# Half of an attention layer's probability tiles turned by DMA in place of TensorE

## What is computed

```python
xn = layernorm(x)                               # x: 8 x 512 x 256, float32
q, k, v = split(xn @ qkv_w.T)                   # 16 heads of 64
q, k = rope(q), rope(k)
scores = q @ k.T / 8 - p * log1p(a * |i - j|)   # p, a per head
attn = softmax(scores)                          # 512 x 512 for each batch and head
y = (attn @ v) @ out_w.T
x = x + y + moe(xn)                             # 16 experts, top 1, capacity 256
```

## Time and profile before

| | us |
|---|---|
| median of 3 runs | 1337.12 |
| lowest, highest | 1335.97, 1337.2 |
| the profiled execution | 1339.31 |
| its span | 1337.5 |
| TensorE busy in the span | 1216.2 (91%) |
| VectorE | 1098.9 (82%) |
| ScalarE | 985.9 (74%) |
| GpSimd | 798.0 (60%) |

### The profile page before, as it was taken

How to read it: one execution, slowest core, us unless ns; L and a number is a source line. 1 busy time by engine, 2 the same in 40 slices (tenths; PEclk the granted TensorE clock), 3 DMA queues, 4 the chain that set the end, 5 groups by cost and what they waited for, 6 DMA issues and landing times.

```text
span 1337.5 us, 33943 instructions
## 1 busy us (share of the span) xinstructions
PE 1216.2 (91%) x13412; PEld 938.0 (70%) x13412; DVE 1098.9 (82%) x2166; ACT 985.9 (74%) x1831; POOL 798.0 (60%) x628
## 2 busy tenths in 40 slices
PE   5630999997699999999999999999999999999995
PEld 5620788895267777777777777777777777777764
DVE  7864799994388888888888888888888888888894
ACT  2775688882388777777778777877778777877773
POOL 3044000001788887886788788877778887886600
PEclk9975899998899999999999999999999999999998
DMA  8625666661445444444553454355445444444411
GB/s 267 237 62 187 219 236 234 234 212 40 117 123 141 104 111 127 120 117 115 147 154 98 112 151 104 96 141 142 117 130 146 105 112 127 120 118 113 135 41 48
DMA packets 172685, 182.47 MB, mean 136 GB/s; under 512 B 78066, under 2 KB 150783, under 8 KB 172528
## 3 DMA queue, kind: packets, MB, share of 16 engines
q1 hardware_dynamic: 160256, 160.03, 41.9%
q0 software_dynamic: 4352, 12.41, 2.7%
q10 hardware_dynamic: 7920, 7.87, 2.0%
HBM read 109.12 MB, written 54.56 MB: 122 GB/s over the span
## 4 chain that ended last, share of the span: by engine, by line
PE 71%; ACT 1%; DMA 1%; issue 1%; DVE 1%; SPq 0%; ACTq 0%; DVEq 0%
PE ps_t L1307 17%; PE ps_o L1323 13%; PE ps_x L1263 13%; PE ps_s L1296 8%; PE ps_s L1297 8%; PE ps_x L1283 7%; PE ps_x L1273 6%; ACT prob L1111 1%; DMA kswap<-qk_dram 0%; DMA qk_dram<-parts 0%; DMA ot<-ctx_parts 0%; ACT proj L1073 0%; ACT prob L1073 0%; DVE ctx_parts L1193 0%; ACT pt_hi L1087 0%
## 5 line engine op out<-in xcount | busy, mean ns | idle before, releaser
L1172 DVE SCALAR_TENSOR_TENSOR pt_lo<-ps_t,pt_hi 128x1024 f16<-128x1024 f32 x256 | 312.6, 1221 | 129.1 <-ACT pt_hi L1087 129.1
L1207 DVE CUSTOM_DVE_ANT_0 neg<-ps_s,strips,score_scale 128x512 f32<-128x512 f32 x512 | 361.7, 743 | 8.1 <-PE ps_s L1297 8.0
L1111 ACT ACTIVATE prob<-neg,neg_max 128x512 f32<-128x512 f32 x512 | 362.6, 712 | 0.0
L1087 ACT ACTIVATE pt_hi<-ps_t 128x1024 f16<-128x1024 f32 x256 | 261.9, 1023 | 128.5 <-PE ps_t L1307 126.5
L1307 PE MATMUL ps_t<-ident,prob 128*128 128x128 f32 x2048 | 269.4, 273 | 4.3 <-ACT prob L1111 4.2
L1307 PEld LDWEIGHTS ps_t<-ident,prob 128*128 128x128 f32 x2048 | 234.3, 141 | 39.1 <-issue 10.6
L1323 PE MATMUL ps_o<-val_hi,pt_hi 128*128 128x64 f16 x2048 | 206.0, 193 | 1.8 <-DVE pt_lo L1172 1.7
L1323 PE MATMUL ps_o<-val_hi,pt_lo 128*128 128x64 f16 x2048 | 206.2, 193 | 0.0
L1323 PE MATMUL ps_o<-val_lo,pt_hi 128*128 128x64 f16 x2048 | 206.2, 193 | 0.0
L1296 PE MATMUL ps_s<-qk 128*128 128x512 f16 x512 | 195.4, 382 | 6.0 <-DMA kswap<-qk_dram 5.6
L1297 PE MATMUL ps_s<-kswap,qk 128*128 128x512 f16 x512 | 194.9, 381 | 0.0
(11 more groups left out here) (186 smaller groups left out, 2565.0 us busy)
## 6 DMA issues: line engine op xcount, KB each, us to landing
raw<-in_L_ffn_w_dram SPq DMA_DIRECT2D x32, 1024.0 KB, 5.1
qk_dram<-parts SPq DMA_DIRECT2D x128, 256.0 KB
qk<-qk_dram SPq DMA_DIRECT2D x32, 1024.0 KB, 5.6
kswap<-qk_dram SPq DMA_DIRECT2D x64, 256.0 KB, 6.5
xa<-in_L_attn_x_dram SPq DMA_DIRECT2D x8, 512.0 KB, 6.4
xt_dram<-xth SPq DMA_DIRECT2D x8, 512.0 KB, 5.1
slots_dram<-zeros SPq DMA_DIRECT2D x4, 1024.0 KB, 8.3
xa<-slots_dram SPq DMA_DIRECT2D x16, 256.0 KB, 5.3
```

Source lines behind the costliest of these rows:

```text
L1087: nc.scalar.activation(pt[0][:, (l - 1) % 2].rearrange("p q k c -> p q (k c)"), ps_t[l % 2][:], ACT.Copy, scale=P_SCALE).then_inc(turned_h ...
L1111: nc.scalar.activation(prob[:, l % 2, q, :], neg[:, l % 2, q, :], ACT.Exp, bias=neg_max[:, 2 * (l % 2) + q:2 * (l % 2) + q + 1], scale=-1. ...
L1172: nc.vector.scalar_tensor_tensor(out=pt[1][:, (l - 1) % 2].rearrange("p q k c -> p q (k c)"), in0=ps_t[l % 2][:], scalar=P_SCALE, in1=pt[0 ...
L1207: nc.vector.tensor_tensor_reduce(neg[:, l % 2, q, :], ps_s[q][:], strips[:, h, start:start + S], score_scale[:, 0:1], 3.0e38, ALU.add, ALU ...
```

## The change

- In the odd slots but the last (127 of 256) the probabilities are not transposed by TensorE. ScalarE splits off their high half from `prob` into `prob_parts` (`prob_high`), VectorE the low half (`prob_low`, in slot s+1), and SP turns both in one DMA transpose of 2048 float16 a partition into `pt` (`turn_probs`). `prob_parts` has one buffer. The even slots go through TensorE as before.
- The values of a slot are taken three slots later, not two; `pair_lo` of a slot three slots later.
- `neg` is gone: reductions write to `prob` and the exponentials work in place, in a ring of three. `pt` has three buffers and holds both halves.
- `rot` holds one of the two rotations, so `step` splits each right after it is rotated. In the first two fills VectorE does so too.
- SP's list is written by groups, with `move` in two halves, `move_out` at the start of the next group and `move_in` after the second turn in it, and the context's transpose after the third.

The diff, cut to its core:

```diff
+DMA_TURNS = (1, 3, 5, 7)
...
-        rot = sb("rot", [P, 2, 2, S])
+        rot = sb("rot", [P, 2, S])
...
-        neg = sb("neg", [P, 2, 2, S])
         neg_max = sb("neg_max", [P, 4])
-        prob = sb("prob", [P, 2, 2, S])
+        prob = sb("prob", [P, 3, 2, S])
         sums = sb("sums", [P, 2, 8])
         rsum = sb("rsum", [P, 8])
-        pt = [sb(f"pt_{n}", [P, 2, 2, TPB, P], F16) for n in ("hi", "lo")]
+        pt = sb("pt", [P, 3, 2, 2, TPB, P], F16)
+        prob_parts = sb("prob_parts", [P, 2, 2, S], F16)
...
+        def by_dma(s):
+
+            return s % 8 in DMA_TURNS and s < NB * PAIRS - 2
+
+        def dma_slots(s):
+
+            return sum(by_dma(i) for i in range(s))
+
+        def pe_slots(s):
+
+            return s - dma_slots(s)
...
-            def move(n, r):
+            def move_out(n, r):
 
                 F = 2 * n + r
-                wait(sp, scored, 16 * (F - 1))
                 sp.wait_ge(parts_lo, 2 * F + 2)
                 for h in range(HG):
                     sp.dma_start(qk_dram[r, :, :, :, :, h, :].rearrange("w a f d s -> d (w a f) s"),
                                  parts[32 * h:32 * h + 32].rearrange("p w a f s -> p (w a f) s")).then_inc(parts_written, 16)
+
+            def move_in(n, r):
...
+            def turn_probs(s):
+
+                n = dma_slots(s)
+                wait(sp, pv_done, s - 2)
+                sp.wait_ge(prob_lo, n + 1)
+                sp.dma_start_transpose(pt[:, s % 3].rearrange("p a q k c -> p (a q k) c"),
+                                       prob_parts[:].rearrange("p a q s -> p (a q s)")).then_inc(turned_by_dma, 16)
...
+            def group(b, j):
+                first = PAIRS * b + 8 * j
+                before = divmod(4 * b + j - 1, 4)
+                if first:
+                    turn_probs(first - 1)
+                    if ahead(*before):
+                        move_out(*ahead(*before)[:2])
+                turn_probs(first + 1)
+                if first + 8 < NB * PAIRS:
+                    move_in((4 * b + j + 1) // 2, (j + 1) % 2)
+                if j == 1 and not is_last(b):
+                    load_routes(b + 1)
+                turn_probs(first + 3)
+                if first:
+                    turn_context(*before)
+                turn_probs(first + 5)
+                if j == 1 and not is_last(b):
+                    sp.wait_ge(filled, fills_before(b, 14))
+                    load_x(b + 1)
...
             def step(F, fills):
                 for w in range(2):
                     rotate(F, w, fills + 2 * w + 2)
-                for w in range(2):
                     if F > 1:
                         high(F, w)
                     low(F, w)
...
             def pair_hi(b, l):
-                act.wait_ge(turned, pairs_turned(b, l))
-                wait(act, pv_done, PAIRS * b + l - 2)
-                nc.scalar.activation(pt[0][:, (l - 1) % 2].rearrange("p q k c -> p q (k c)"), ps_t[l % 2][:],
+                s = PAIRS * b + l - 1
+                act.wait_ge(turned, pe_slots(s) + 1)
+                wait(act, pv_done, s - 2)
+                nc.scalar.activation(pt[:, s % 3, 0].rearrange("p q k c -> p q (k c)"), ps_t[pe_slots(s) % 2][:],
                                      ACT.Copy, scale=P_SCALE).then_inc(turned_hi, 1)
 
-            def context_hi(b, l):
-
-                unit = PAIRS // 4 * b + (l - 6) // 4
-                two = (l - 6) // 4 % 2
+            def prob_high(s):
+                n = dma_slots(s)
+                act.wait_ge(exp_done, 2 * s + 2)
+                wait(act, turned_by_dma, 16 * n)
+                nc.scalar.activation(prob_parts[:, 0], prob[:, s % 3], ACT.Copy, scale=P_SCALE).then_inc(prob_hi, 1)
...
+                if s % 4 == 3 and s >= 7:
+                    context_hi(s // 4 - 1)
                 if kind:
                     read_fill(kind, fills_before(b, l))
-                if l or not is_first(b):
-                    pair_hi(b, l)
                 for q in range(2):
                     act.wait_ge(negated, 2 * s + q + 1)
-                    if q == 0:
-                        wait(act, turned, pairs_turned(b, l - 1))
-                    nc.scalar.activation(prob[:, l % 2, q, :], neg[:, l % 2, q, :], ACT.Exp,
+                    nc.scalar.activation(prob[:, s % 3, q, :], prob[:, s % 3, q, :], ACT.Exp,
                                          bias=neg_max[:, 2 * (l % 2) + q:2 * (l % 2) + q + 1], scale=-1.0,
                                          accum_out=sums[:, l // 4 % 2, 2 * (l % 4) + q:2 * (l % 4) + q + 1]).then_inc(exp_done, 1)
-                if l % 4 == 2 and not (is_first(b) and l == 2):
-                    context_hi(b, l)
+                if by_dma(s):
+                    prob_high(s)
+                if s and not by_dma(s - 1):
+                    pair_hi(b, l)
...
-            def pair_lo(b, l):
-                dve.wait_ge(turned_hi, pairs_turned(b, l))
-                nc.vector.scalar_tensor_tensor(out=pt[1][:, (l - 1) % 2].rearrange("p q k c -> p q (k c)"), in0=ps_t[l % 2][:],
-                                               scalar=P_SCALE, in1=pt[0][:, (l - 1) % 2].rearrange("p q k c -> p q (k c)"),
+            def pair_lo(s):
+                dve.wait_ge(turned_hi, pe_slots(s) + 1)
+                nc.vector.scalar_tensor_tensor(out=pt[:, s % 3, 1].rearrange("p q k c -> p q (k c)"), in0=ps_t[pe_slots(s) % 2][:],
+                                               scalar=P_SCALE, in1=pt[:, s % 3, 0].rearrange("p q k c -> p q (k c)"),
                                                op0=ALU.mult, op1=ALU.subtract).then_inc(turned_lo, 1)
 
-            def read_context(b, l):
-
-                unit = PAIRS // 4 * b + (l - 6) // 4
-                two = (l - 6) // 4 % 2
-                dve.wait_ge(pv_done, PAIRS * b + l - 2)
+            def prob_low(s):
+                dve.wait_ge(prob_hi, dma_slots(s) + 1)
+                nc.vector.scalar_tensor_tensor(out=prob_parts[:, 1], in0=prob[:, s % 3], scalar=P_SCALE, in1=prob_parts[:, 0],
+                                               op0=ALU.mult, op1=ALU.subtract).then_inc(prob_lo, 1)
...
+                if s % 2 and s >= 3:
+                    pair_lo(s - 3)
+                if s % 4 == 0 and s >= 8:
+                    context_lo(s // 4 - 2)
+                if s % 4 == 3 and s >= 7:
+                    read_context(s // 4 - 1)
                 for q in range(2):
                     start = SW - S - (2 * (l % 2) + q) * P
                     dve.wait_ge(scored, 2 * s + q + 1)
+                    if q == 0 and s >= 3:
+                        if by_dma(s - 3):
+                            dve.wait_ge(prob_lo, dma_slots(s - 2))
+                        else:
+                            dve.wait_ge(turned, pe_slots(s - 2))
                     wait(dve, exp_done, 2 * s - 3 + q)
                     i = 2 * (l % 2) + q
-                    nc.vector.tensor_tensor_reduce(neg[:, l % 2, q, :], ps_s[q][:], strips[:, h, start:start + S],
+                    nc.vector.tensor_tensor_reduce(prob[:, s % 3, q, :], ps_s[q][:], strips[:, h, start:start + S],
                                                    score_scale[:, 0:1], 3.0e38, ALU.add, ALU.min,
                                                    neg_max[:, i:i + 1]).then_inc(negated, 1)
+                if s and by_dma(s - 1):
+                    prob_low(s - 1)
                 kind = slot_kind(b, l)
                 if kind:
                     read_fill(kind, b, l, fills_before(b, l))
-                if l or not is_first(b):
-                    pair_lo(b, l)
-                if l % 4 == 3 and not (is_first(b) and l == 3):
-                    context_lo(b, l - 1)
...
             def turn_first(w):
 
                 dve.wait_ge(x_free, 2 * w + 2)
                 if w:
-                    dve.wait_ge(turned_parts, 6)
+                    dve.wait_ge(parts_lo, 1)
                 for i, (half, table) in enumerate(((0, cos), (1, sin), (0, sin), (1, cos))):
                     nc.vector.tensor_tensor(prod0[:, i, :], proj0[:, w, half, :], table[:], ALU.mult).then_inc(turned_parts, 1)
                 dve.wait_ge(turned_parts, 6 * w + 4)
-                nc.vector.tensor_tensor(rot[:, w, 0, :], prod0[:, 0, :], prod0[:, 1, :], ALU.subtract).then_inc(turned_parts, 1)
-                nc.vector.tensor_tensor(rot[:, w, 1, :], prod0[:, 2, :], prod0[:, 3, :], ALU.add).then_inc(turned_parts, 1)
-
-            turn_first(0)
-            turn_first(1)
+                nc.vector.tensor_tensor(rot[:, 0, :], prod0[:, 0, :], prod0[:, 1, :], ALU.subtract).then_inc(turned_parts, 1)
+                nc.vector.tensor_tensor(rot[:, 1, :], prod0[:, 2, :], prod0[:, 3, :], ALU.add).then_inc(turned_parts, 1)
+
             for w in range(2):
+                turn_first(w)
                 dve.wait_ge(parts_hi, w + 1)
...
-                wait(pe, turned_lo, pairs_turned(b, l - 2))
+                n = pe_slots(s - 1)
```

(72 more changed lines are left out.)

24 lines of the change are left out of this document (14 added, 10 removed).

## The result

The changed kernel takes 1470.14 us (median; 1465.79 to 1478.55), the kernel before 1337.16: a ratio of 1.0986, 95% interval 1.0917 to 1.1055. It is slower by 132 us, where 1322 was forecast and the range ended at 1358.

What follows compares the result with a forecast made beforehand. The bound was to move from TensorE to VectorE: a group of 25.2 + 2.7 + 1.1 + 0.5 = 29.5 us instead of 30.08; with start and end, -15.1 in all, giving 1322.0 us; 8-in-10 range 1262 to 1358.

Steps and rivals of the forecast that it cites:

- TensorE's saving: Odd slots lose their eight transposes on TensorE: 3.5 us a group, so TensorE alone would need 26.6.
- VectorE's solid work: Reductions, low halves and other VectorE operations of a group, before any wait: 25.2 us.
- VectorE against GpSimd: Four `prob_low` and two `context_lo` a group wait on GpSimd operations, 0.45 us each: 2.7 us, between 0 and 5.6.
- The loop is 0.1 + 3.7 + ...: `prob_high`, `prob_low` and the DMA landing through one `prob_parts` buffer: 6.1 us, making VectorE wait 1.1 once a group.
- I take 0.5, between 0 and 1.4: Lateness a group of slot 3's turn, which stands behind `move_in` in SP's in-order list.
- The context's transpose follows it: In SP's list the context's transpose comes after slot 3's turn, itself up to 1.4 us late; no own cost given.
- `move_out` stands behind the turn of slot 7 ... covered: On SP, `move_out` also needs GpSimd's last `parts_lo`, about 2 us into the next group; counted as covered.
- The clock, "2 in 100": Less TensorE work lowers its clock: chance 2 in 100, within the slower case; granted clock expected to stay 1.00.
- Start and end, +3.2: Second rotation waiting for the one `rot` half at the start, +1.4; a low half and extra values at the end, +1.8.
- signs for "right": Transposes x1032, TensorE gaps 2 to 3 us a group, VectorE idle under 3, `prob_low` 1.5 to 1.8, GpSimd mean over 1.4.
- signs for "wrong": `prob_low` at 1.23 throughout with groups of 27, values waiting for the DMA on TensorE, or `prob_high` waiting in every pair.
- The rival *Slower: VectorE's waits on GpSimd, the loop and the turn behind `move_in` pass 4.9 us a group: 1369 us, chance 0.28.

Runs made afterwards that it cites:

- e10: Changed kernel with only slot 7 turned by DMA, `move_out` back at the group's end and `move_in` before slot 1's turn: 1340.39 us, ratio 0.9977.
- e3: Changed kernel with GpSimd's rotations and splits on 8 columns in place of 512: 1464.26 us, ratio 1.0889 to the kernel before.
- e13: Changed kernel with DMA turns cut to 1 of 16 blocks from slot 8 on and GpSimd's operations on 8 columns: 1321.19 us, ratio 0.9884.
- e4: Changed kernel with DMA turns cut to 1 of 16 blocks from slot 8 on: 1361.48 us, ratio 1.0164 to the kernel before.
- e1: Changed kernel with no slot turned by DMA, TensorE transposing all 256, rest of the change kept: 1333.68 us, ratio 0.9938 to the kernel before.
- e8: Changed kernel with one DMA turn a group (slot 7), the other slots by TensorE: 1386.38 us, ratio 1.0281 to the kernel before.
- e11: Changed kernel with only slot 5 turned by DMA, `move_out` at the group's end and `move_in` before slot 1's place: 1378.20 us, ratio 1.0286.

## Why the prediction was wrong, step by step

- **TensorE's saving (3.5 us a group), VectorE's solid work (25.2).** Nothing speaks against them; neither is the bound of the changed kernel. That less work on TensorE comes back as time is seen in one run with whole turns, e10, and there in part.
- **VectorE against GpSimd, 2.7 us a group.** Right in size: (1.746 - 1.22) x 127 + (0.923 - 0.68) x 64 = 82 us over 32 groups, 2.6. Wrong in place: e3, 13 us less with intervals that overlap, shows little or no cost in this kernel, and e13 against e4 that it costs 37 us, half of its size, where the DMA is out of the way.
- **"The loop is 0.1 + 3.7 + ..." and "I take 0.5, between 0 and 1.4".** This is the step that failed. 3.7 was the landing of a transpose alone in the queue. Where ScalarE waited for one of the four new ones, 5.25 us passed in the median, and up to 8.2. By the share of the queue (72.8% after, 41.2% in e1, of 744 us, 21.9 and 24.8 groups) a turn takes 3.1 us of all 16 engines, not 2.2. ScalarE waits for landings twice a group and not once, 2.6 us in all, where 1.1 + 0.5 was taken. e4 gives the price of the size: 110 us.
- **"The context's transpose follows it".** It was seen and not priced. It is TensorE's longest wait, 2.4 us each in 27 groups, with the context's transpose issued late and landing in 3.9.
- **"`move_out` stands behind the turn of slot 7 ... covered".** Only GpSimd was checked as its cover. What the move meets 8 us later was not: e8 against e10, 41 us for one turn.
- **`val_lo` and `yacc`.** That `prob_low` goes ahead of the reading of a fill, which frees `ps_x` for TensorE, was costed at nothing and not named: 47 us in the changed kernel's trace, 40 in e11's.
- **The clock, "2 in 100".** The earlier trace rows had short gaps. After the wait of 3.6 us shown above the clock was at half: the granted clock was 0.94 in the stage, so some 12% of it at half clock. That is at most 0.06 x 744 = 45 us of 744, or at most 2 of the 4 us that a group has grown, and it comes on top of the waits. No run separates it from the waits that bring it.
- **Start and end, +3.2.** The first group took 36.2 us instead of 32.1, and 35.9 in e1, with no turn at all: more than the 1.4 taken for the start, and little beside 132. The last group but one took 33.1, where 26.2 was forecast, since the turns are in it too.
- **Two small sums.** 23.8 + 4 x 0.88 is 27.3 and not 27.6 for GpSimd, and 25.2 + 0.9 + 1.1 + 0.5 is 27.7 and not 27.9 for the period. The forecast rests on neither.

Of the prediction's own signs for "right", the x1032 transposes and a mean of `prob_low` between 1.5 and 1.8 us came. The gaps did not: TensorE idles 5.0 us a group and not 2 to 3 ((744 - 634.5) / 21.9), VectorE 5.6 and not under 3. Of the signs for "wrong", the values on TensorE do wait for the DMA (24.8 us in 18 times), and `prob_high` waits in about every second pair.

The rival *Slower* named the right places, SP's one queue and the one `prob_parts` buffer, at 0.28 and 1369 us. It was short by 100 us. It added up waits on one engine and left out that they meet TensorE's fills, behind which the clock falls as well; how the 100 us are shared between these two no run shows.

The Trainium skill (Advanced Engine Details and Errata, X-Bar Transpose (TRN2)) would have had the turns cheaper still than the rows (350 to 400 GB/s, where the earlier trace rows has 267); the runs go the other way, with 3.1 us of all 16 engines for a turn. Its rule on two SBUF inputs (SBUF — State Buffer, Who interferes with whom) agrees with e3, where `prob_low` falls from 1572 to 1224 ns in the median once GpSimd's operations are short.

## What to carry to other kernels

Price a transfer by the queue that it will stand in, not by its landing alone: count the time of all 16 engines that each transfer takes in a period, and write down for every one what is issued just ahead and just behind it. When a step is moved in an in-order list, look at what the step behind it now collides with, and at what its reader holds up (here a PSUM bank). Where TensorE was full and gets one long wait, look at the granted clock behind it too: here a wait of 3.6 us was followed by 2.9 us lost at half clock.

## What the runs showed of the hardware

A DMA transpose of 512 KB that follows 1.5 MB of plain loads in the same queue (3.1 us behind the first of them in the group shown) held SP for 5.1 us and landed after 7.9 (medians, e8); with 9.4 us between them it held it for 1.6 and landed after 3.7 (medians, e10). A `prob_low` took up to 3.04 us in the changed kernel, where GpSimd's operations are long, and 1.22 where it is alone. TensorE's granted clock was 1.00 when it came to stand still at 726.2, fell to 0.50 near 728.3, while it still stood, and was 1.00 again from 735.1, after 5.4 us of work.
